# First edge layer of a two-layer graph network: 16-bit keys, and the high part of target blocks compared by a distance from ScalarE

## The chip, the cores and the metric

The kernel runs on one core of a Trainium2 chip. Its engines are TensorE (PE, with its weight loads as PEld), VectorE (DVE), ScalarE (ACT), GpSimd (POOL) and SyncE (SP), and 16 DMA engines move data between the device memory and the on-chip memory. The metric is the time of one execution in microseconds.

## The reference, cut to what matters

There are 50,000 nodes with 256 features and 50,000 edges, each with a source `src`, a target `dst` and one of 8 types. `dst` is sorted when it is drawn.

```python
h = relu(layernorm(x))
xt = einsum('ni,rio->rno', h, weight)             # 8 weights of 256x256
messages = xt[edge_type, dst]                     # row edge_index[1] = dst
x = x + relu(segment_sum(messages, src, 50000) + bias)
h = relu(layernorm(x))
h_neigh = h @ W_neigh                             # keep the 32 largest per row
x = x + h @ W_self + segment_sum(maxk(h_neigh)[src], dst) / max(deg, 1)
```

In the first layer the edge reads the row of `dst` and adds into the row of `src`.

## The kernel before, in words

**Tables.** At the start VectorE makes tables of the edges (lines 783 to 888): for each edge its type, source and target as f32, its code, and the slot that it gets when the edges are ordered by type. There are 400 tiles of 128 slots. `key0` holds for each slot the node to which its message is added (up to 50,000). TensorE turns it, and VectorE copies it from PSUM (line 887) to on-chip memory; SP stores it as `key0_rows` in device memory. `bucket_row` and `high_row` (lines 794 to 796) are `dst >> 7` and `dst >> 9` of every edge in f16, stored as `bucket_rows` and `high_rows`.

**The first edge layer.** It runs in 100 steps of 4 tiles (`NBT`, `B`), two steps per turn of a loop, with buffers for even and odd steps. In the step of batch b:
- SP loads the keys of the batch's 512 slots and the next 128, broadcast to 128 partitions (`load_keys0`, line 530).
- GpSimd gathers the rows of `x` for batch b+3 (`gather0`, line 652) and adds the messages of b into `agg` in device memory (`add0`, line 658), in turns: gather, add, gather, add. An add waits for the add two places before it, and for its message.
- VectorE (`edge0_front`, line 911) compares the row of keys with the column of keys of each tile (`pick`, line 920), makes one-hots for a count of degrees, waits for the gathered rows (line 936), copies the next indices `gidx` (line 937) and computes the statistics of the layer norm. When ScalarE has made `std` (line 1226), it computes the scales; `edge0_cross` (line 942) compares keys with those of the next tile (`cross`, line 947); `edge0_back` makes the scatter's indices.
- ScalarE (`edge0_step`, line 1241), for batch b at step b+2: evicts messages 0, 1 and 2 from PSUM (line 1238) with one turned copy between, then computes `std` and the normalised `h` of batch b+2, then the second turned copy and the last eviction.
- TensorE merges equal keys with `pick`, multiplies by the weight of the tile's type, and adds the part that `cross` carries.

**The counting sort beside it.** The second layer needs the edges in order of `dst`. Its sort is spread over the same steps in phases (`PHASES`, line 471): "hist" 13 steps, "rank" 30 steps with 28 chunks of 14 tiles, "sort" 56 steps and "rest" the last 2. In a rank step SP loads the chunk's rows of `bucket_rows` (f16, 1792 per partition, 128 partitions) and `high_rows` (98 partitions) (`load_rank_rows`, line 535). VectorE's `rank_hots` (line 1008) comes at the end of the step, after front, cross, back and `rank_out`: it compares the high part with the number of the partition (line 1011) for `high_of`, a one-hot over 98 partitions; then 14 comparisons of the bucket row with a column, summed (line 1019). TensorE's `rank_choose` (line 1439) looks up the start of each bucket with `high_of`.

**Order.** The order on each engine is written out by hand: `phased` (line 75) and `pipeline` (line 98) call the parts of a step in order, write out the steps at the edges and put the rest in a loop of two steps. ScalarE's part of the edge layer goes through `pipeline`, the other engines' (but GpSimd's) through `phased`. Semaphores are all counted; `wait_from` skips a wait where there is nothing to wait for yet.

After the edge layer come the node layer (98 steps) and the summing of the second layer, which the change does not touch.

Of the kernel before, what the change touches and what calls it, by code (L numbers as in the profile page):

```python
# [20 lines left out]
F32 = mybir.dt.float32  # L21
F16 = mybir.dt.float16
# [52 lines left out]
def phased(eng, phases, first, last, body):  # L75

    t = 0
    for phase, count, looped in phases:
        lo, hi = max(t + 4, first), min(t + count - 4, last)
        pairs = max(0, (hi - lo) // 2) if looped else 0  # L80
        u = t
        while u < t + count:
            if pairs and u == lo:
                with eng.Fori(0, pairs) as i:
                    body(phase, At(i, lo), At(i, lo - t))
                    body(phase, At(i, lo + 1), At(i, lo + 1 - t))
                u += 2 * pairs
            else:
                body(phase, At(None, u), At(None, u - t))
                u += 1  # L90
        t += count


def inside(b, nb):
    return not isinstance(b, int) or 0 <= b < nb


def pipeline(eng, nb, *parts):

    deepest = max(lag for _, lag in parts)
    first, last = 2 + deepest, nb - 3 + deepest % 2

    def step(i, t):
        for part, lag in parts:
            b = t - lag
            if i is not None:
                part(i * 2 + b, i + b // 2, b % 2)
            elif 0 <= b < nb:  # L110
                part(b, b // 2, b % 2)

    for t in range(first):
        step(None, t)
    with eng.Fori(0, (last + 1 - first) // 2) as i:
        step(i, first)
        step(i, first + 1)
    for t in range(last + 1, nb + deepest):
        step(None, t)


def wait_from(eng, sem, value, batch, first):

    if not isinstance(batch, int) or batch >= first:
        eng.wait_ge(sem, value)
# [18 lines left out]
def graph_layers(nc, x, src, dst, etype, w_rel, bias, w_self, w_neigh, out):  # L144
    agg = nc.dram_tensor("agg", [ROWS, D], F32).ap()
    hs = nc.dram_tensor("hs", [NPAD, D], F32).ap()
    key0_rows = nc.dram_tensor("key0_rows", [(SLOTS + 1) * P], F32).ap()
    bucket_rows = nc.dram_tensor("bucket_rows", [SLOTS * P], F16).ap()
    high_rows = nc.dram_tensor("high_rows", [SLOTS * P], F16).ap()

    ctx = ExitStack()
    with ctx:
        def sb(name, shape, dt=F32):
            return ctx.enter_context(nc.sbuf_tensor(name, shape, dt))

        def sem(name):
            return ctx.enter_context(nc.semaphore(name))
# [51 lines left out]
        rawf = {n: view(zone_b, (3 + k) * COLS, [COLS // P, P]) for k, n in enumerate(NAMES)}  # L209
        tab = {n: sb(f"tab_{n}", [P, COLS]) for n in NAMES}  # L210
        bucket_row = sb("bucket_row", [P, COLS // P, P], F16)
        high_row = sb("high_row", [P, COLS // P, P], F16)
        tmp_i = sb("tmp_i", [P, COLS], I32)
        tmp_f = sb("tmp_f", [P, COLS])
        code16 = sb("code16", [P, COLS], U16)
# [27 lines left out]
        def two(name, shape, dt=F32):  # L243
            return [sb(f"{name}{p}", shape, dt) for p in range(2)]

        def two_views(zone, at, shape, dt=F32):
            words = 1
            for n in shape:
                words *= n
            words = words if dt in (F32, I32) else words // 2  # L250
            return [view(zone, at + p * words, shape, dt) for p in range(2)]
# [4 lines left out]
        msg = two("msg", [P, B * D])  # L256
        pick = [[sb(f"pick{p}{j}", [P, P]) for j in range(B)] for p in range(2)]
        cross = [[sb(f"cross{p}{j}", [P, P]) for j in range(B)] for p in range(2)]
        keyrow = two("keyrow", [P, BE + P])
        gidx = two("gidx", [P, B], I32)  # L260
        sidx = two("sidx", [P, B], I32)
        keycol = two("keycol", [P, B])
# [53 lines left out]
        one_low = two_views(zone_c, DEGREES, [B, P], F16)  # L316
        one_high = two_views(zone_c, DEGREES + B * P, [B, TILES], F16)
        bucket_in = two_views(zone_c, RANK, [RC * P], F16)
        high_in = two_views(zone_c, RANK + RC * P, [RC * P], F16)
        low_pick = two_views(zone_c, RANK + 2 * RC * P, [RC, LO], F16)  # L320
        rank_junk = view(zone_a, 0, [RC, P], F16)
        high_of = two_views(zone_a, RC * P // 2, [RC * P], F16)
# [114 lines left out]
        starts_ready = sem("starts_ready")  # L437
        rank_rows_in = pair("rank_rows_in")
        rank_col = sem("rank_col")
        rank_hot = sem("rank_hot")  # L440
        earlier_done = sem("earlier_done")
        chosenmm = sem("chosenmm")
# [46 lines left out]
        def _(sp):  # L489
# [24 lines left out]
            def store_rows(dram, tile, tiles, done):  # L514
                whole = tiles // P
                v = dram[0:whole * P * P].rearrange("(c r p) -> r c p", r=P, p=P)
                sp.dma_start(v, tile[:, 0:whole, :]).then_inc(done, 16)
                sp.dma_start(dram[whole * P * P:tiles * P].rearrange("(r p) -> r p", p=P),
                             tile[0:tiles - whole * P, whole, :]).then_inc(done, 16)

            sp.wait_ge(rawf_done, 1)
            store_rows(bucket_rows, bucket_row, SLOTS, rank_rows_stored)
            store_rows(high_rows, high_row, SLOTS, rank_rows_stored)
            sp.wait_ge(keyT_done, 1)
            store_rows(key0_rows, rawf["src"], SLOTS + 1, key0_stored)
            sp.wait_ge(key0_stored, 32)
            sp.wait_ge(rank_rows_stored, 64)


            def load_keys0(b, r, p):  # L530
# [3 lines left out]

            def load_rank_rows(c, r, p):
                wait_from(sp, earlier_done, c - 1, c, 2)
                wait_from(sp, rank_hot, c - 1, c, 2)
                at = bass.ds(c * (RC * P), RC * P)
                sp.dma_start(bucket_in[p], bucket_rows[at].unsqueeze(0).to_broadcast([P, RC * P])
                             ).then_inc(rank_rows_in[p], 16)  # L540
                sp.dma_start(high_in[p][0:HI, :], high_rows[at].unsqueeze(0).to_broadcast([HI, RC * P])
                             ).then_inc(rank_rows_in[p], 16)

            def edge0_loads(phase, at, chunk):
# [226 lines left out]
        def _(dve):  # L771
            count = [0]

            def link(ins):

                count[0] += 1
                ins.then_inc(own, 1)
                dve.wait_ge(own, count[0])
# [12 lines left out]
            dve.wait_ge(raw_in, 16 * 9)  # L791
            for n in NAMES:
                link(v.tensor_copy(rawf[n][:, :, :], raw[n][:, :, :]))
            for shift_by, rows16 in ((7, bucket_row), (9, high_row)):
                link(v.tensor_scalar(raw["type"][:, :, :], raw["dst"][:, :, :], shift_by, None, ALU.arith_shift_right))
                link(v.tensor_copy(rows16[:, :, :], raw["type"][:, :, :]))
            v.memset(key0[:, SLOTS:COLS], float(N)).then_inc(rawf_done, 1)
            for k, n in enumerate(NAMES):
                dve.wait_ge(pe_done, k + 1)
# [71 lines left out]
            def decode(coded, to, n):  # L871
# [12 lines left out]
            link(v.tensor_tensor(key0[:, s], key0[:, s], tmp_f[:, s], ALU.add))  # L884
            v.tensor_copy(tmp_f[:, 0:1], key0[:, 0:1]).then_inc(dve_ready, 1)
            dve.wait_ge(pe_done, 5)
            v.tensor_copy(rawf["src"][:, :, :], bank[4][:, :].rearrange("p (c q) -> p c q", q=P)
                          ).then_inc(keyT_done, 1)


# [115 lines left out]
                dve.wait_ge(starts_ready, 1)  # L1006

            def rank_hots(c, rc, p):
                dve.wait_ge(rank_rows_in[p], 32 * (rc + 1))
                wait_from(dve, chosenmm, c - 1, c, 2)  # L1010
                v.tensor_scalar(high_of[p][0:HI, :], high_in[p][0:HI, :], part_f[0:HI, 0:1], None, ALU.is_equal
                                ).then_inc(rank_hot, 1)
                wait_from(dve, rank_own, 4 * (c - 1), c, 2)
                v.tensor_tensor(low_pick[p], iota_h[:, 0:LO].unsqueeze(1).to_broadcast([P, RC, LO]),
                                low16[:, bass.ds(c * RC, RC)].unsqueeze(2).to_broadcast([P, RC, LO]), ALU.is_equal)
                v.tensor_copy(bucket_col[p][:, :], bucket[:, bass.ds(c * RC, RC)]).then_inc(rank_col, 1)
                dve.wait_ge(rank_col, c + 1)
                for j in range(RC):
                    last = v.scalar_tensor_tensor(rank_junk[:, j, :], bucket_in[p][:, j * P:(j + 1) * P],
                                                  bucket_col[p][:, j:j + 1], upto[:, :], ALU.is_equal, ALU.mult,  # L1020
                                                  accum_out=earlier[p][:, j:j + 1])
                last.then_inc(earlier_done, 1)
# [192 lines left out]
        def _(act):  # L1215
# [19 lines left out]
            def edge0_evict(b, p, j):  # L1235
                wait_from(act, added0[j], 16 * (b - 1), b, 2)
                act.wait_ge(msgmm0, b * B + j + 1)
                nc.scalar.copy(msg[p][:, j * D:(j + 1) * D], bank[4 + j % 2][:, j // 2 * D:(j // 2 + 1) * D]  # L1238
                               ).then_inc(msg0, 1)

            def edge0_step(b, r, p):

                turn = not isinstance(b, int) or b + 1 < NBT
                front = not isinstance(b, int) or b + 2 < NBT
                edge0_evict(b, p, 0)
                if turn:
                    edge0_turned(b + 1, 1 - p, 0)
                edge0_evict(b, p, 1)
                edge0_evict(b, p, 2)
                if front:  # L1250
                    edge0_front(b + 2, p)
                if turn:
                    edge0_turned(b + 1, 1 - p, 1)
                edge0_evict(b, p, 3)
# [19 lines left out]
            edge0_turned(0, 0, 0)  # L1274
            edge0_front(1, 1)
            edge0_turned(0, 0, 1)
            pipeline(act, NBT, (edge0_step, 2))


            edge0_over(act)  # L1280
# [315 lines left out]
```

## Time and profile before

| | |
|---|---|
| median of 3 runs | 3609.3 us (3604.76 to 3609.43) |
| the profiled execution | 3607.24 us |
| its span | 3605.5 us |
| busy: DVE, PE, POOL, ACT | 87%, 72%, 68%, 63% |
| mean traffic of the DMA engines | 160 GB/s |
| chain that ended last | DVE 50%, issue 21%, PE 11%, DMA 8% |

The profile is one execution. Busy times are those of each engine over the span, and they overlap. The chain follows, from the last instruction back, what released each piece of work; "issue" is time in which an engine waited for nothing that the profile shows. An idle time before an instruction is put down to what ended it. Times in a timeline are microseconds from the start of the span.

### The profile page before, as it was taken

The numbers are of one execution on the slowest core, as the hardware profiler recorded it, in microseconds if no ns is written. First come the engines' busy times: TensorE is split into PE (matmuls) and PEld (weight loads), VectorE is DVE, ScalarE is ACT, GpSimd is POOL, SyncE is SP. The second block draws the span as 40 slices with busy tenths as digits, with TensorE's granted clock in tenths as the row PEclk, the third lists the DMA queues.
The fourth block names the chain that finished last, engine by engine and source line by source line (L and its number), as shares of the span: only waits on it lengthen the run. The fifth ranks groups of instructions, "written<-read, shape, count | busy, mean of one in ns | idle before, by whom it ended". The sixth has DMA issues, their size and how long they took to land.

```text
span 3605.5 us, 69112 instructions
## 1 busy us (share of the span) xinstructions
PE 2593.9 (72%) x10738; PEld 1677.9 (47%) x10739; DVE 3119.8 (87%) x13785; ACT 2257.1 (63%) x6394; POOL 2450.8 (68%) x1732
## 2 busy tenths in 40 slices
PE   2665666767788888888677777777777765766676
PEld 1224655555566666666333333333333334555454
DVE  8998788888899999999699999999999995666666
ACT  3994233333333333333588888888888867777787
POOL 0003877767787777777688888888888855656665
PEclk9997888888999999999899899998988988889999
DMA  9601466666555555555344444444444437777776
GB/s 368 248 0 48 83 123 144 147 143 149 110 108 104 104 100 103 105 102 100 109 173 164 182 166 171 178 163 177 173 164 182 166 121 244 257 242 258 247 251 218
DMA packets 308041, 576.38 MB, mean 160 GB/s; under 512 B 32095, under 2 KB 188034, under 8 KB 307982
## 3 DMA queue, kind: packets, MB, share of 16 engines
q1 hardware_dynamic: 212366, 419.40, 33.2%
q0 software_dynamic: 95616, 156.31, 22.3%
q8 instruction: 23, 0.38, 0.0%
q14 instruction: 36, 0.29, 0.0%
HBM read 316.70 MB, written 258.88 MB: 160 GB/s over the span
## 4 chain that ended last, share of the span: by engine, by line
DVE 50%; issue 21%; PE 11%; DMA 8%; POOL 4%; DVEq 3%; ACT 2%; POOLq 0%; ACTq 0%; SPq 0%
DVE zone_c L1176 7%; DVE w L1176 7%; DVE best L1169 6%; DVE zone_c L1204 5%; DMA agg<-msg,sidx 5%; PE banks L1569 5%; DMA w<-hs,gidx 3%; PE banks L1469 2%; DVE zone_c L858 2%; DVE zone_c L1049 2%; DVE zone_c L1047 2%; DVE stats L893 2%; DVE zone_c L860 2%; DVE zone_c L1051 2%; POOL rows_in L653 2%
## 5 line engine op out<-in xcount | busy, mean ns | idle before, releaser
L1541 PE MATMUL banks<-w,hT 128*128 128x512 f32 x1568 | 795.4, 666 | 199.8 <-ACT hT L1321 195.1
L665 POOL DMA_INDIRECT agg<-msg,sidx x400 | 665.3, 1663 | 206.4 <-issue 111.9
L653 POOL DMA_INDIRECT rows_in<-in_x,gidx x400 | 421.8, 1054 | 435.7 <-DVE gidx L909 305.3
L1541 PEld LDWEIGHTS banks<-w,hT 128*128 128x128 f32 x1568 | 325.7, 213 | 613.3 <-issue 500.6
L1204 DVE SCALAR_TENSOR_TENSOR zone_c<-banks,rdeg,zone_c 128x256 f32 x784 | 379.4, 484 | 245.8 <-PE banks L1569 201.0
L1569 PE MATMUL banks<-w,zone_c 128*128 x1568 | 428.1, 429 | 208.4 <-DVE zone_c L1204 99.5
L732 POOL DMA_INDIRECT w<-hs,gidx x392 | 371.3, 947 | 230.3 <-DMA w<-hs,gidx 90.6
L1411 PE MATMUL banks<-pick,h 128*128 128x128 f32 x1600 | 287.1, 307 | 311.8 <-ACT h L1220 218.8
L1469 PE MATMUL banks<-w,hT 128*128 x1600 | 481.1, 429 | 18.3 <-issue 17.1
L1238 ACT COPY msg<-banks 128x256 f32<-128x256 f32 x400 | 148.0, 370 | 510.6 <-PE banks L1480 497.3
L1569 PEld LDWEIGHTS banks<-w,zone_c 128*128 128x128 f32 x1568 | 316.1, 212 | 320.6 <-issue 275.2
L1411 PEld LDWEIGHTS banks<-pick,h 128*128 128x128 f32 x1600 | 256.1, 215 | 374.5 <-issue 352.2
L1347 ACT ACTIVATE zone_c<-zone_c,ones 128x128 f32<-128x128 f32 x784 | 305.9, 390 | 134.7 <-PE banks L1569 132.7
L1169 DVE MAX8 best<-zone_c 128x8 f32<-128x256 f32 x980 | 341.9, 411 | 0.0
L1469 PEld LDWEIGHTS banks<-w,hT 128*128 128x128 f32 x1600 | 308.6, 214 | 63.7 <-issue 32.6
L709 POOL TENSOR_TENSOR zone_c<-msg,zone_c 128x1024 f32<-128x1024 f32 x98 | 232.8, 2375 | 149.2 <-ACT zone_c L1309 149.2
L1176 DVE MATCH_REPLACE8 zone_c<-best,zone_c 128x256 f32<-128x256 f32 x784 | 311.9, 409 | 0.0
L1341 ACT ACTIVATE zone_c<-iota_f,minus_key 128x128 f32<-128x128 f32 x784 | 302.6, 386 | 4.7 <-DMA hs<-zone_c 4.6
L698 POOL TENSOR_SCALAR zone_c<-zone_c 128x1024 f32<-128x1024 f32 x98 | 272.0, 2775 | 7.0 <-DMA zone_c<-agg 7.0
L1480 PE MATMUL banks<-msg,cross 128*128 128x256 f32 x798 | 261.4, 412 | 0.0
L1226 ACT ACTIVATE std<-mv,eps 128x4 f32<-128x4 f32 x100 | 29.7, 297 | 345.7 <-DVE mv L897 345.7
L703 POOL TENSOR_TENSOR zone_c<-rows_in,zone_c 128x1024 f32<-128x1024 f32 x98 | 235.6, 2404 | 8.6 <-POOL zone_c L698 0.2
(233 smaller groups left out, 5841.6 us busy)
## 6 DMA issues: line engine op xcount, KB each, us to landing
out_rows<-zone_c SPq DMA_DIRECT2D x196, 512.0 KB, 2.7
agg<-bias SPq DMA_DIRECT2D x2, 25344.0 KB, 97.3
zone_c<-agg SPq DMA_DIRECT2D x98, 512.0 KB, 5.4
hs<-zone_c SPq DMA_DIRECT2D x98, 512.0 KB, 3.6
zone_c<-out_rows SPq DMA_DIRECT2D x98, 512.0 KB, 6.0
rows_in<-in_x SPq DMA_DIRECT2D x97, 512.0 KB, 4.6
keyrow<-key_rows SPq DMA_DIRECT2D x100, 320.0 KB, 4.0
zone_c<-bucket_rows SPq DMA_DIRECT2D x28, 448.0 KB
```

The source lines that it names most:

```text
L653: pool.indirect_dma_start(out=rows_in[p][:, j, :], out_offset=None, in_=x[:, :], in_offset=bass.IndirectOffsetOnAxis(ap=gidx[p][:, j:j + 1 ...
L665: pool.indirect_dma_start(out=agg[:, :], out_offset=bass.IndirectOffsetOnAxis(ap=sidx[p][:, j:j + 1], axis=0), in_=msg[p][:, j * D:(j + 1) ...
L732: pool.indirect_dma_start(out=ring[:, k, :], out_offset=None, in_=hs[:, :], in_offset=bass.IndirectOffsetOnAxis(ap=gidx1[p][:, k:k + 1], a ...
L1169: last = v.max(best[:, j, :], (work if k else neigh)[p][:, j, :])
L1176: last = v.match_replace(work[p][:, j, :], best[:, j, :], (work if k else neigh)[p][:, j, :], NEG)
L1204: ins = v.scalar_tensor_tensor(to, bank[k % 8][:, 0:D], node, to, ALU.mult, ALU.add)
L1341: nc.scalar.activation(near[:, k % 4, :], iota_f[:, 0:P], ACT.Abs, bias=minus_key[:, bass.ds(s, 1)]).then_inc(near1, 1)
L1347: nc.scalar.activation(hot1[:, k % HOTS, :], near[:, k % 4, :], ACT.Relu, bias=ones[:, 0:1], scale=-1.0).then_inc(hot1_done, 1)
L1411: last = mm(bank[j // 2][:, k * P:(k + 1) * P], h[p][:, j, c * P:(c + 1) * P], pick[p][j][:, 0:P], start=True, stop=True)
L1469: last = mm(to, hT[p][:, j // 2, k * P:(k + 1) * P], w0[:, bass.ds(rel, 1), c, :].rearrange("k r d -> k (r d)"), start=(c == 0), stop=alon ...
L1541: last = mm(bank[4 + j][:, :], hT[p][:, c, j * P:(j + 1) * P], w1[:, c, :], start=(c == 0), stop=(c == KC - 1))
L1569: mm(bank[k % 8][:, 0:D], hot1[:, k % HOTS, :], ring_cols[:, bass.ds(words[k], D)], start=True, stop=True).then_inc(steps1, 1)
```

## The change

- `key0_rows` and both `keyrow` buffers hold unsigned 16-bit integers. The copy from PSUM writes a new tile `key16`. The load per step is half as many bytes; the comparisons at lines 920 and 947 read 16-bit input, and their outputs stay f32.
- `high_row`, `high_rows` and the load of it are gone. In its place ScalarE computes |bucket - (4 p + 1.5)| from the bucket row on 98 partitions (`rank_distance`), with a per-partition bias `high_mid`, and VectorE compares it with 2: a bucket belongs to the high part p when it is 4p, ..., 4p+3.
- `rank_distance` stands in ScalarE's step between the third eviction and `edge0_front`. VectorE waits for it in `rank_hots`. SP waits for it (`rank_near`), in place of VectorE's comparison, before it loads over a bucket row. ScalarE waits for the bucket row and for the comparison two chunks back.
- ScalarE's edge layer goes through `phased`, so that it knows the chunk; its last step is written behind it.

```diff
-    key0_rows = nc.dram_tensor("key0_rows", [(SLOTS + 1) * P], F32).ap()
+    key0_rows = nc.dram_tensor("key0_rows", [(SLOTS + 1) * P], U16).ap()
-    high_rows = nc.dram_tensor("high_rows", [SLOTS * P], F16).ap()
-        high_row = sb("high_row", [P, COLS // P, P], F16)
+        high_mid = sb("high_mid", [P, 1])
+        key16 = sb("key16", [P, COLS // P, P], U16)
-        keyrow = two("keyrow", [P, BE + P])
+        keyrow = two("keyrow", [P, BE + P], U16)
-        high_in = two_views(zone_c, RANK + RC * P, [RC * P], F16)
+        high_near = two_views(zone_c, RANK + RC * P, [RC * P], F16)
...
-            store_rows(high_rows, high_row, SLOTS, rank_rows_stored)
             sp.wait_ge(keyT_done, 1)
-            store_rows(key0_rows, rawf["src"], SLOTS + 1, key0_stored)
+            store_rows(key0_rows, key16, SLOTS + 1, key0_stored)
...
             def load_rank_rows(c, r, p):
                 wait_from(sp, earlier_done, c - 1, c, 2)
-                wait_from(sp, rank_hot, c - 1, c, 2)
+                wait_from(sp, rank_near, c - 1, c, 2)
                 at = bass.ds(c * (RC * P), RC * P)
                 sp.dma_start(bucket_in[p], bucket_rows[at].unsqueeze(0).to_broadcast([P, RC * P])
-                             ).then_inc(rank_rows_in[p], 16)
-                sp.dma_start(high_in[p][0:HI, :], high_rows[at].unsqueeze(0).to_broadcast([HI, RC * P])
                              ).then_inc(rank_rows_in[p], 16)
...
-            for shift_by, rows16 in ((7, bucket_row), (9, high_row)):
-                link(v.tensor_scalar(raw["type"][:, :, :], raw["dst"][:, :, :], shift_by, None, ALU.arith_shift_right))
-                link(v.tensor_copy(rows16[:, :, :], raw["type"][:, :, :]))
+            link(v.tensor_scalar(raw["type"][:, :, :], raw["dst"][:, :, :], 7, None, ALU.arith_shift_right))
+            link(v.tensor_copy(bucket_row[:, :, :], raw["type"][:, :, :]))
+            v.tensor_scalar(high_mid[:, :], part_f[:, :], -float(LO), -(LO - 1) / 2, ALU.mult, ALU.add)
...
-            v.tensor_copy(rawf["src"][:, :, :], bank[4][:, :].rearrange("p (c q) -> p c q", q=P)
+            v.tensor_copy(key16[:, :, :], bank[4][:, :].rearrange("p (c q) -> p c q", q=P)
...
             def rank_hots(c, rc, p):
-                dve.wait_ge(rank_rows_in[p], 32 * (rc + 1))
+                dve.wait_ge(rank_rows_in[p], 16 * (rc + 1))
                 wait_from(dve, chosenmm, c - 1, c, 2)
-                v.tensor_scalar(high_of[p][0:HI, :], high_in[p][0:HI, :], part_f[0:HI, 0:1], None, ALU.is_equal
-                                ).then_inc(rank_hot, 1)
+                dve.wait_ge(rank_near, c + 1)
+                v.tensor_scalar(high_of[p][0:HI, :], high_near[p][0:HI, :], LO / 2, None, ALU.is_lt).then_inc(rank_hot, 1)
...
+            def rank_distance(c, rc, p):
+                act.wait_ge(rank_rows_in[p], 16 * (rc + 1))
+                wait_from(act, rank_hot, c - 1, c, 2)
+                nc.scalar.activation(high_near[p][0:HI, :], bucket_in[p][0:HI, :], ACT.Abs, bias=high_mid[0:HI, 0:1]
+                                     ).then_inc(rank_near, 1)
+
-            def edge0_step(b, r, p):
+            def edge0_step(b, p, chunk):
...
                 edge0_evict(b, p, 2)
+                if chunk is not None:
+                    rank_distance(*chunk)
                 if front:
                     edge0_front(b + 2, p)
...
-            pipeline(act, NBT, (edge0_step, 2))
+
+            def edge0_body(phase, at, chunk):
+                b, _, p = at.back(2)
+                c, rc, pc = chunk.back(0)
+                if inside(b, NBT):
+                    edge0_step(b, p, (c, rc, pc) if phase == "rank" and inside(c, RCHUNKS) else None)
+
+            phased(act, PHASES, 2, NBT, edge0_body)
+            edge0_step(NBT - 1, 1, None)
```

## Rows read from the trace of the kernel before

**Rows 1.** Busy us by stretch (start:end, length), engines; then PEclk, DMA share, GB/s.
```profile
520.00:930.00 410.00, 286.14 (x1589) 236.42 (x1590) 349.19 (x2146) 132.78 (x305) 290.64 (x219) 0.84 0.68 146
930.00:1640.00 710.00, 586.19 (x3048) 450.50 (x3047) 645.63 (x3421) 254.81 (x584) 557.45 (x428) 0.94 0.57 104
```

**Rows 2.** Timeline of DVE, line 937, rank: start, us, instruction, [idle before <-what ended it].
```profile
528.94 0.16 DVE L937 COPY gidx<-from 128x4 int32<-128x4 int32 x1
...
756.97 0.17 DVE L937 COPY gidx<-from 128x4 int32 x1 [4.07 <-DMA rows_in<-in_x,gidx]
...
918.87 0.17 DVE L937 COPY gidx<-from 128x4 int32<-128x4 int32 x1 [1.40 <-DMA rows_in<-in_x,gidx]
```

**Rows 3.** Waits in rank (first), then hist: total us, times, longest.
```profile
DVE gidx L937 <- DMA rows_in<-in_x,gidx: 27.9, 24, 4.1
...
DVE pick L920 <- DMA keyrow<-key_rows: 15.3, 4, 5.8
```

**Rows 4.** Timeline of one rank step, picked from SP, POOL, DVE and ACT.
```profile
698.31 0.33 SPq L532 DMA_DIRECT2D keyrow<-key_rows  x1
699.00 0.33 SPq L539 DMA_DIRECT2D zone_c<-bucket_rows  x1
699.13 1.66 POOL L665 DMA_INDIRECT agg<-msg,sidx  x1 [0.30 <-issue]
...
704.43 1.02 POOL L653 DMA_INDIRECT rows_in<-in_x,gidx  x1 [0.30 <-issue]
708.79 1.58 POOL L665 DMA_INDIRECT agg<-msg,sidx  x1 [3.33 <-DMA agg<-msg,sidx]
709.31 0.17 DVE L937 COPY gidx<-from 128x4 int32 x1 [1.15 <-DMA rows_in<-in_x,gidx]
...
711.35 0.30 ACT L1226 ACTIVATE std<-mv,eps 128x4 f32<-128x4 f32 x1 [4.02 <-DVE mv L897]
```

**Rows 5.** Chain of waits over 520 to 940: shares by line; one piece (start, us).
```profile
by line: DMA agg<-msg,sidx 35.8%; issue 25.9%; POOL rows_in L653 10.6%; PE banks L1469 7.1%; POOL agg L665 6.5%; PE banks L1411 4.1%; PE banks L1480 3.1%; DMA rows_in<-in_x,gidx 1.5%; ACT h L1220 1.3%; PE banks L1419 1.0%; DVE stats L893 0.
...
699.13 8.74 DMA agg<-msg,sidx
```

**Rows 6.** Timeline of POOL in sort, two adds two places apart.
```profile
1203.10 1.58 POOL L665 DMA_INDIRECT agg<-msg,sidx  x1 [0.30 <-issue]
...
1210.05 1.64 POOL L665 DMA_INDIRECT agg<-msg,sidx  x1 [0.30 <-issue]
```

**Rows 7.** Busy time of a short stretch in rank, columns as in rows 1.
```profile
700.00:707.00 7.00, 7.00 (x34) 5.54 (x34) 6.91 (x47) 1.37 (x4) 4.54 (x4) 0.79 0.99 234
```

**Rows 8.** DMA in rank: SP's queue (packets, MB, share); the key load's us to landing.
```profile
q1 hardware_dynamic: 10944, 31.05, 27.7%
...
keyrow<-key_rows SPq DMA_DIRECT2D x28, 320.0 KB, 4.5
```

**Rows 9.** Groups of DVE's instructions in rank: busy us, mean ns of one.
```profile
L1019 DVE SCALAR_TENSOR_TENSOR zone_a<-zone_c,bucket_col,upto 128x128 f16<-128x128 f16 x392 | 109.2, 347 | 1.0
...
L920 DVE SCALAR_TENSOR_TENSOR pick<-keyrow,keycol,upto 128x128 f32<-128x128 f32 x110 | 32.2, 348 | 1.9 <-DVE keycol L915 0.5
...
L947 DVE TENSOR_SCALAR_CACHE_REDUCE cross<-keyrow,livekey 128x128 f32<-128x128 f32 x110 | 31.6, 343 | 1.3
L927 DVE TENSOR_SCALAR zone_c<-iota_h,lowcol 128x128 f16<-128x128 f16 x108 | 27.7, 256 | 0.0
```

**Rows 10.** Groups of ACT's instructions over the span: busy us, mean ns of one.
```profile
L1341 ACT ACTIVATE zone_c<-iota_f,minus_key 128x128 f32<-128x128 f32 x784 | 302.6, 386 | 4.7 <-DMA hs<-zone_c 4.6
...
L1329 ACT ACTIVATE w<-w,minus_one 128x512 f32<-128x512 f32 x98 | 70.8, 722 | 50.2 <-DVE w L1176 47.0
```

**Rows 11.** ACT in rank: its wait before `std` in total, and the shortest in the timeline.
```profile
ACT std L1226 <- DVE mv L897: 94.4, 27, 7.3
...
530.97 0.30 ACT L1226 ACTIVATE std<-mv,eps 128x4 f32<-128x4 f32 x1 [1.29 <-DVE mv L897]
```

**Rows 12.** Timeline of DVE near the start.
```profile
10.87 0.43 DVE L796 CAST high_row<-zone_b 128x512 f16<-128x512 int32 x1
```

More of the change, by code:

```diff
@@ L439, in graph_layers @@
         rank_col = sem("rank_col")
+        rank_near = sem("rank_near")
         rank_hot = sem("rank_hot")
@@ L522, in _ @@
             store_rows(bucket_rows, bucket_row, SLOTS, rank_rows_stored)
-            store_rows(high_rows, high_row, SLOTS, rank_rows_stored)
             sp.wait_ge(keyT_done, 1)
-            store_rows(key0_rows, rawf["src"], SLOTS + 1, key0_stored)
+            store_rows(key0_rows, key16, SLOTS + 1, key0_stored)
             sp.wait_ge(key0_stored, 32)
-            sp.wait_ge(rank_rows_stored, 64)
+            sp.wait_ge(rank_rows_stored, 32)
             def load_keys0(b, r, p):
```

## Prediction

> **What bounds the kernel now.** I read the page first, then the busy time by stretch, with the first edge layer cut at its phases. Tables are built until 313 us; then come "hist" (to about 520), "rank" (to about 930), "sort" (to about 1640) and a short rest. Rank and sort are what the reader should compare [rows 1]. Each of rank's 28 chunks loads two kinds of bucket rows, which sort doesn't. Vector and GpSimd are both close to their limit there, so the question is which wait ends last.
>
> The distance between the copies of `gidx` gives one step: in rank, from 528.94 to 918.87 in 26 steps, 15.0 us each [rows 2]. Vector waits 27.9 us in 24 places for gathered rows of `x` [rows 3]. GpSimd issues four gathers and four scatter-adds per step. In the step shown [rows 4] an add starts at 699.13, the one two places on at 708.79, after an idle time of 3.33 us that a scatter ended: an add waits for the one two places back. The gather at 704.43 lands late behind the same traffic, and Vector waits for it until 709.31. The chain of waits agrees: the largest entry of the rank stretch is scatters under way, 35.8%, and the piece in that step runs 8.74 us from start to landing [rows 5]. In sort, two adds that are two places apart start 6.95 us apart, and no scatter ends the idle time before the later one [rows 6]. So rank is bound by scatters that land late, with Vector near behind; sort is bound by Vector, which is busy for 645.6 of 710 us [rows 1].
>
> Why late? SP issues the key load at 698.31, the buckets at 699.00 and then the high parts [rows 4], just ahead of the slow scatter. From 700 to 707 the DMA engines are 99% busy at 234 GB/s [rows 7], against 68% over the stretch [rows 1]. Burst and scatter share the engines.
>
> **The high rows go, and the keys halve.** In rank SP's queue moved 31.05 MB in 27.7% of 410 us [rows 8]: 113.6 us of all engines, 3.66 us per MB. The high load is 98 rows of 3584 bytes, 0.351 MB: 1.28 us. Half of the keys' 320 KB is 0.164 MB: 0.60 us. Together 1.88 us leave each burst, of the 4.2 us that its three loads (1.14 MB) cost. The scatter of 8.74 us would land after 6.9 if it moves by the whole of that. GpSimd itself needs an add, a gather and two issue gaps, twice, between two such adds: 2 x (1.58+0.30+1.00+0.30) = 6.4 us [rows 4, 6]. So most of a stall of 2 to 3 us goes, about 1.9 us in a period of 15.0. Next late is Vector: its step without the gather wait is 15.0 - 27.9/26 = 13.9 us, and there the gain stops. Bounds: 27.9 us, and nothing, if the scatter is late for another reason. I take 24 us, since the longest wait, 4.07 us [rows 2], exceeds what 1.9 us take off, and a few like it leave some 4 us.
>
> In hist Vector waits 15.3 us in four places for keys [rows 3]. That is latency more than volume: keys land after 4.5 us in rank [rows 8], of which the halved bytes are 0.60. Four times 0.6 is 2.4; I take 2, bounds 0 and 15.3. In sort I take 0: its steps are bound by Vector's own work.
>
> **Compares on 16-bit keys.** `pick` (L920) takes 348 ns with f32 input; the same instruction at L1019 with 16-bit input and output takes 347 [rows 9]. So 0. For `cross` (L947, 343 ns) no row shows a 16-bit form. The nearest single-input compare with 16-bit on both sides is L927, 256 ns, without a sum. Bounds: 0, and 400 x 0.087 = 35 us less. I take 0, since the output and the sum stay f32 and L1019 gains nothing even with both sides at 16-bit.
>
> **The distance on ScalarE.** ACT takes 386 ns for 128 elements and 722 for 512 [rows 10]: 0.875 ns each, so 1792 elements take 722 + 1280 x 0.875 = 1842 ns. It stands after the third eviction and ahead of `std`, for which Vector waits; the normalising of `h`, a turned copy and the fourth eviction are queued behind it, and PE and GpSimd's fourth add wait for those. ACT sits idle just there: 94.4 us in rank's 27 steps, 3.5 in the mean, 1.29 in the shortest [rows 11], the only one of them under 1.84. That costs 0.55 us once; I take 1 for all, since steps that were held up by gathers lose some cover. The distance needs its bucket row, issued at 699.00, for the idle time that begins at 711.35 - 4.02 = 707.33 [rows 4], 8.3 us later; keys land in 4.5 [rows 8]. Vector's new wait for the distance comes after its wait for `std`, which follows the distance on ACT: no stall. SP's wait for the distance two chunks back ends before the wait beside it (`earlier_done`), so its queue, keys included, isn't delayed; it issues one DMA less. If the cover is gone, each step costs up to 1.84 us.
>
> The Trainium skill ("ScalarE: Activation LUTs", Rules for kernel authors) advises keeping simple arithmetic off ScalarE, which it puts at up to three times slower per element. The formula in its section What ACT_TABLE_LOAD costs gives an estimate of 1.77 us for this instruction, near the 1.84 from the rows. By the rule the edit is a loss, at most the rival of the late `std` below; the trace speaks against it here, since the idle time hides the length.
>
> **Rank's compare.** L1011 keeps shape and types, with a number in place of a [98,1] operand, and one wait instruction more. I take 0; as bounds, an estimate of the 87 ns between L947 and L927 for either way, 28 x 0.087 = 2.4 us less or more.
>
> **The start.** A shift and a cast of 128x512 go, 0.43 us each [rows 12], and a [128,1] operation comes, well under half of one. Vector works alone for most of the time up to 313 us: -0.8 us, bounds -0.9 and -0.5. The key store, in half the bytes but in runs of 256 bytes instead of 512, stands before the first key load: 0, bounds -1 and +1. ScalarE's loop is written out per phase as the other engines' are; ACT is busy 132.8 of 410 us [rows 1], which hides it: 0, at worst +3 at the edges of phases.
>
> **Sum.** -24 - 2 - 0.8 + 1 = -26 us. The profiled execution took 3607.24 us, span 3605.5, and would take 3581. The median of the runs shown, 3609.3, lies 2 us above it, so I forecast 3583 us.
>
> **Rivals.**
> - *The volume was not the cause.* The scatter stands behind the bucket load, which stays, or GpSimd's own order keeps it late. For it: the larger of the row loads keeps its place. Against: the burst loses 45% of its bytes. Kept are the start and some of the rest, 1 to 7 us: 3605. Chance 0.15.
> - *The distance delays `std`* (the slower side). A bucket row that lands late puts the distance in front of `std`. It decides at 711.35 - 1.84 = 709.5, 10.5 us after the issue: every microsecond beyond costs one per step. Full price 28 x 1.84 = 52 us, less the 26 gained: 3635; it is slower than before once over half of each distance is exposed. For it: the burst still fills the engines to 707. Against: 3.5 us of mean idle time, and fewer bytes ahead. Chance 0.07.
> - *`cross` gets faster.* Up to 35 us on Vector; GpSimd's period of 4 x 3.18 = 12.7 us lies under Vector's by enough to let most of it through. Some 30 more: 3553. For it: a compare at 256 ns exists. Against: L1019. Chance 0.08.
> - *The forecast*, with its own range of 3574 to 3595. Chance 0.70.
>
> Less than about 0.2%, 7.2 us, can't be told from no change. Faster by more: 0.70 + 0.08 + 0.02 of the first rival = 0.80. Same: 0.12 of the first rival. Slower: 0.07 + 0.01 = 0.08. The range takes in the first rival up to 3604 and reaches toward the third: 3565 to 3604.
>
> **What would show it.** Right: hardly any idle time of GpSimd in rank that a scatter ends; Vector's gather wait there below 6 us; steps of 13.9 to 14.1 us with the chain through Vector; a distance of 1.8 us inside ACT's idle time; L920 and L947 unchanged; sort as long as before. Wrong: scatters still over 7 us from start to landing; Vector waiting longer for `std`; L947 under 300 ns. The forecast fails above all if the scatters' landing doesn't move.

## The result and the profile after

| | before | after |
|---|---|---|
| median | 3608.2 us (3604.8 to 3609.4, 4 runs) | 3575.1 us (3574.6 to 3576.8, 4 runs) |
| ratio, 95% interval | | 0.9911 [0.9893, 0.9928] |
| span of the profiled execution | 3605.5 us | 3573.5 us |
| mean granted clock of TensorE | 0.904 | 0.906 |

The change makes the kernel faster, by 0.9%. 3583 us was forecast, 8 us above the result, which lies in the range. The page of after has the same engines at the top. In the chain that ended last the DMA engines have 3% and Vector 57% (8% and 50% before), and the key load is half as large.

```profile
DVE 57%; issue 20%; PE 11%; DVEq 4%; DMA 3%; POOL 2%; ACT 2%; POOLq 0%; ACTq 0%; SPq 0%
...
keyrow<-key_rows SPq DMA_DIRECT2D x100, 160.0 KB, 3.6
zone_c<-bucket_rows SPq DMA_DIRECT2D x28, 448.0 KB, 5.3
```

Busy time of after in rank and in sort, columns as in [rows 1]. The stretch taken for rank is 27 us shorter, its ends rounded to fit each trace; Vector does the same work in it (347 us) and is now busy for 91% of it, against 85%. The DMA share falls from 0.68 to 0.61.

```profile
520.00:903.00 383.00, 279.10 (x1582) 231.45 (x1583) 346.87 (x2128) 176.41 (x328) 290.42 (x222) 0.86 0.61 120
903.00:1612.00 709.00, 592.45 (x3090) 455.10 (x3089) 647.14 (x3451) 256.54 (x587) 561.90 (x428) 0.94 0.54 92
```

Waits of after in rank (total us, times, longest). The wait for gathered rows, 27.9 us in [rows 3], is 0.5. GpSimd waited 32.3 us in 13 places for scatters before; now 2.0 in two. What holds an add back now is its message from ScalarE (28.4 us; 22.9 before).

```profile
DVE gidx L935 <- DMA rows_in<-in_x,gidx: 0.5, 1, 0.5
...
POOL agg L663 <- DMA agg<-msg,sidx: 2.0, 2, 1.1
...
POOL agg L663 <- ACT msg L1236: 28.4, 30, 1.7
...
ACT std L1224 <- DVE mv L895: 28.3, 21, 2.7
...
DVE rstd L900 <- ACT std L1224: 10.2, 27, 0.7
```

The chain through rank, by line. In [rows 5] scatters under way were its largest entry, 35.8%; they aren't among the entries that the line shows any more, and Vector's lines lead.

```profile
by line: DVE zone_a L1017 18.2%; issue 14.5%; DVE stats L891 7.2%; PE banks L1483 6.8%; DVE pick L918 6.5%; DVE cross L945 6.4%; DVE zone_c L926 5.4%; PE banks L1425 4.4%; DVE zone_c L925 3.5%; PE banks L1494 3.2%; DVE mv L895 2.1%; ACT std
```

A rank step of after, picked from four engines; compare [rows 4]. The distance (L1242) ends at 796.42, 0.81 us before `std` begins, so it lies in idle time. The add at 801.62 waits for its message, not for a scatter.

```profile
794.63 1.79 ACT L1242 ACTIVATE zone_c<-zone_c,high_mid 98x1792 f16<-98x1792 f16 x1
...
795.18 0.17 DVE L935 COPY gidx<-from 128x4 int32 x1
...
797.23 0.30 ACT L1224 ACTIVATE std<-mv,eps 128x4 f32<-128x4 f32 x1 [0.81 <-DVE mv L895]
...
799.32 0.33 SPq L532 DMA_DIRECT2D keyrow<-key_rows  x1
...
801.62 1.73 POOL L663 DMA_INDIRECT agg<-msg,sidx  x1 [1.37 <-ACT msg L1236]
```

Vector's instructions in rank that read the keys, and the compare of the distance (busy us, mean ns). They answer to [rows 9]: 349 for 348 ns, and 343 for 343. L1010, with a number in place of a [98,1] operand, took 694 ns before.

```profile
L918 DVE SCALAR_TENSOR_TENSOR pick<-keyrow,keycol,upto 128x128 f32<-128x128 uint16 x108 | 31.7, 349 | 1.4
L945 DVE TENSOR_SCALAR_CACHE_REDUCE cross<-keyrow,livekey 128x128 f32<-128x128 uint16 x108 | 31.0, 343 | 1.2
L1010 DVE TENSOR_SCALAR zone_a<-zone_c 98x1792 f16<-98x1792 f16 x28 | 17.8, 635 | 2.8 <-issue 0.4
```

**Where 32 us of span went.** The copies of `gidx`, one per step and numbered here from 0, are landmarks in both traces. After leads by 1.3 us at the first, by 1.2 at number 13 (the first step of rank), by 25.6 at number 41 (behind rank's last chunk), by 29.9 at 43 (the first step of sort) and by 32.7 at the last. So hist gave nothing, rank's chunks 24.4 us, the two steps from 41 to 43, with neither a chunk of rank nor one of sort, 4.2, the rest of the edge layer some 3, and what follows it nothing (the lead is 32.0 at the end). The stretches called sort in [rows 1] and above begin ahead of these two.

### The profile page after: what moved, and what is told of

Its sections match the earlier page's. It is cut to its first block, busy times and chain, and to the rows that moved or that the text cites. A ratio compares the mean times of both kernels' runs of the same rounds, so it can differ in the third digit from the quotient of the medians.

```text
span 3573.5 us, 69007 instructions
## 1 busy us (share of the span) xinstructions
PE 2582.5 (72%) x10738; PEld 1668.3 (47%) x10739; DVE 3115.5 (87%) x13784; ACT 2306.0 (65%) x6422; POOL 2444.8 (68%) x1732
## 3 DMA queue, kind: packets, MB, share of 16 engines
q0 software_dynamic: 95616, 156.31, 22.9%
## 4 chain that ended last, share of the span: by engine, by line
DVE 57%; issue 20%; PE 11%; DVEq 4%; DMA 3%; POOL 2%; ACT 2%; POOLq 0%; ACTq 0%; SPq 0%
DVE zone_c L1174 7%; DVE w L1174 7%; DVE best L1167 6%; DVE zone_c L1202 5%; PE banks L1583 4%; DVE stats L891 3%; PE banks L1483 3%; DMA w<-hs,gidx 3%; DVE pick L918 3%; DVE cross L945 2%; DVE zone_c L1045 2%; DVE zone_c L926 2%; DVE zone_c L856 2%; DVE zone_c L1047 2%; DVE zone_c L1049 2%
## 5 line engine op out<-in xcount | busy, mean ns | idle before, releaser
L1218 ACT ACTIVATE h<-rows_in,shift,rstd 128x256 f32<-128x256 f32 x400 | 207.3, 588 | 44.2 <-DVE shift L902 44.2
```

## The experiments

Each run is compared with the kernel before on the same chip. From the last copy of `gidx` to the end, which no edit touches, the traces take 1890 to 1980 us, so only ratios and stretches are compared across chips. "Rank" is the mean of 22 steps between copies of `gidx` (numbers 17 to 39); "turn" is the next six steps, from rank's last two chunks into sort; "sort" is the mean of 50 steps (46 to 96). Each is read from one trace; the two of the changed kernel differ by 0.03 us a step in rank, 0.5 in the turn and 0.02 in sort.

| run | ratio to before | rank, us a step | turn, us | sort, us a step |
|---|---|---|---|---|
| before | | 14.94 | 83.3 | 13.36 |
| after | 0.9911 [0.9893, 0.9928] | 14.14 | 77.9 | 13.30 |
| a0_after | 0.9916 [0.9898, 0.9934] | 14.11 | 77.4 | 13.28 |
| k1_keys_only | 0.9988 [0.9979, 0.9997] | 14.89 | 82.3 | 13.32 |
| k2_distance_only | 0.9917 [0.9903, 0.9930] | 14.19 | 77.8 | 13.18 |
| k9_full_traffic | 0.9991 [0.9977, 1.0005] | 15.04 | 82.8 | 13.30 |
| k8_own_rows | 0.9982 [0.9970, 0.9994] | 14.86 | 83.3 | 13.32 |
| k3_load_put_back | 0.9935 [0.9922, 0.9949] | 14.48 | 81.0 | 13.16 |
| k11_half_load | 0.9951 [0.9934, 0.9968] | 14.55 | 83.1 | 13.24 |
| k10_rows_later | 0.9920 [0.9898, 0.9942] | 14.18 | 78.1 | 13.34 |
| k12_rows_later_keys16 | 0.9931 [0.9915, 0.9948] | 14.18 | 77.6 | 13.33 |
| k5_distance_twice | 0.9965 [0.9951, 0.9978] | 14.75 | 80.2 | 13.20 |
| k6_distance_last | 1.0053 [1.0035, 1.0071] | 15.82 | 82.6 | 13.22 |
| k7_bucket_col_on_act | 0.9925 [0.9907, 0.9942] | 13.94 | 77.2 | 13.47 |

**Which part: the keys alone.** The kernel before with 16-bit keys and nothing else.

```diff
-    key0_rows = nc.dram_tensor("key0_rows", [(SLOTS + 1) * P], F32)
+    key0_rows = nc.dram_tensor("key0_rows", [(SLOTS + 1) * P], U16)
...
-        keyrow = two("keyrow", [P, BE + P])
+        keyrow = two("keyrow", [P, BE + P], U16)
...
```

> The kernel before with 16-bit keys alone: the load of the high rows and its comparison on VectorE stay. Theory A (the bytes of the burst of loads delay one scatter-add per rank step): 0.60 of the 1.88 us of DMA time per burst goes, so GpSimd's idle time on scatters in rank falls by about a third from 55 us (scatter and message together), Vector's wait for gathered rows from 27.9 to about 17 us, and the whole kernel is 8 to 14 us faster, 3 of it at the start of the sort phase. Rival B (only the third load, behind the buckets, is what the scatter stands behind): rank keeps its 15.0 us steps, and no more than 4 us are gained. Rival C (16-bit input speeds the comparison of the sort phase): the sort phase is over 10 us shorter and L947 is under 330 ns.

Some 4 us of 3660, and rank's steps hardly move. Its waits in 310 us of rank (560 to 870) show the stall still there. The first fence is of this run, the second of before in the same stretch.

```profile
POOL agg L666 <- DMA agg<-msg,sidx: 20.1, 9, 3.5
...
DVE gidx L938 <- DMA rows_in<-in_x,gidx: 17.7, 17, 3.4
```

```profile
POOL agg L665 <- DMA agg<-msg,sidx: 26.5, 11, 3.3
...
DVE gidx L937 <- DMA rows_in<-in_x,gidx: 19.9, 18, 4.1
```

**Which part: the distance alone.** After, with keys as f32 again (the diff above the other way round).

> The changed kernel with f32 keys again: the high rows are not loaded, ScalarE makes the distance. Theory A: 1.28 of 1.88 us of DMA time per burst goes, enough to take the scatter's landing under the 6.4 us that GpSimd needs anyway in most steps: rank steps of 14.0 to 14.3 us, Vector's gather wait under 8 us, 20 to 28 us faster than before. Rival B (the third load is all): the same rank stretch as in the changed kernel, 24 us less than before, and the keys' part is only in the start of sort. Rival D (gains need both parts, since the wait vanishes only under a threshold): under 12 us faster.

It gives as much as the whole change, and the same two waits are all but gone:

```profile
DVE gidx L934 <- DMA rows_in<-in_x,gidx: 0.7, 1, 0.7
...
POOL agg L662 <- DMA agg<-msg,sidx: 3.5, 3, 1.2
```

**After again**, on the chip of k8_own_rows, k9_full_traffic and k7_bucket_col_on_act.

> The changed kernel again, beside the runs with parts of it, so that ratios and stretches stand on one chip. Every theory: 0.989 to 0.993 of the time before, rank steps (17 to 39) of 14.1 to 14.2 us, as in the two profiles compared so far.

0.9916 on another chip, with rank at 14.11: the result holds.

**The load put back, without its use.** After, and SP loads 98 x 1792 numbers into a tile that nobody reads, from `bucket_rows`; Vector waits for them.

```diff
+                sp.dma_start(unread[p][0:HI, :], bucket_rows[at].unsqueeze(0).to_broadcast([HI, RC * P])
+                             ).then_inc(unread_in[p], 16)
...
+                dve.wait_ge(unread_in[p], 16 * (rc + 1))
```

> The changed kernel with one more load per rank chunk, 98 rows of 3584 bytes as the high rows were, right behind the bucket load, into a tile that nothing reads; VectorE waits for its landing where it waits for the bucket row. Theory A (bytes in the burst): GpSimd's idle time on scatters comes back, rank steps rise from 14.0 to 14.5 or more, and the kernel is 12 to 22 us slower than the changed one, so 11 to 21 us faster than the one before. Rival E (what helped was not the load but the shorter comparison with a number, 59 ns, or ScalarE's new loop): within 3 us of the changed kernel.

Rank 14.48: under half of the 0.75 us that k1_keys_only has over after. Either ScalarE's part has a worth of its own, or this load isn't the old one. It reads the rows that the load just ahead of it reads.

**The same load from rows of its own.** As the last, with a second copy of the bucket rows stored at the start.

```diff
-                sp.dma_start(unread[p][0:HI, :], bucket_rows[at].unsqueeze(0).to_broadcast([HI, RC * P])
+                sp.dma_start(unread[p][0:HI, :], high_rows[at].unsqueeze(0).to_broadcast([HI, RC * P])
...
```

> As the one with a load put back, but the load that nothing reads comes from rows of its own in device memory, as the high rows did, so its three loads move the same bytes between the same places as those of the kernel with 16-bit keys alone, whose rank steps took 14.89 us; with the load from the bucket rows they took 14.48. Theory G (where the bytes come from matters: a second read of the same rows is cheaper): 14.8 to 14.9 us a step, 8 to 10 us slower than the load from the bucket rows. Theory H (it doesn't; what separates 14.48 from 14.89 is who compares, and when VectorE and ScalarE run): 14.4 to 14.6 us again.

14.86, as in k1_keys_only with the same traffic and no distance. SP's queue (packets, MB, share of 16 engines over 310 us of rank), k3_load_put_back first and then this run:

```profile
q1 hardware_dynamic: 8719, 21.19, 23.0%
```

```profile
q1 hardware_dynamic: 8400, 20.45, 26.3%
```

That is 0.230 x 310 / 21.19 = 3.36 us of all engines per MB, against 3.99, for the whole of SP's queue. The two runs differ only in the rows that the third load reads and in the store of them at the start, so reading the same rows again was the cheaper load, 14.48 against 14.86 us a step. How it is cheaper is not shown: the time per MB is not the load's own price, for k10_rows_later below, whose loads all read rows of their own, has 0.268 x 310 / 24.76 = 3.36 as well.

**The whole traffic of before, with the distance.** As the last, with f32 keys.

> The changed kernel with f32 keys and the load that nothing reads from rows of its own: the loads of the kernel before, byte for byte, with the distance on ScalarE. Theory A in its strict form (the bytes of the burst alone set rank's steps): 14.9 to 15.1 us a step, within 4 us of the kernel before. Theory H (a part of the gain is not bytes): 14.6 to 14.7 us a step, 6 us or more faster than before.

Ratio 0.9991, and its interval holds 1; rank 15.04. With the bytes back the gain is gone, so it came from the load that left, and the distance costs or gives less than this can tell. Halving the keys beside the full load is worth 15.04 - 14.86 = 0.18 us a step with the distance and 14.94 - 14.89 = 0.05 without it; once the load is out, 14.19 - 14.11 = 0.08.

**Half of the load.** k8_own_rows with 49 partitions in place of 98.

> The changed kernel with the load that nothing reads from rows of its own, on 49 partitions instead of 98: half the dose of the kernel that had 14.86 us a rank step, against 14.13 with none. Linear in bytes: 14.5 us. Threshold (a landing that stays under the 6.4 us which GpSimd needs anyway costs nothing): 14.1 to 14.25 us, and idle time of GpSimd on scatters under 5 us between 560 and 870, against 23.1 with the full load.

14.11 with none, 14.55 with half, 14.86 with all: each half costs, the first 0.44 us and the second 0.31. Half of the load is not under a size that would be free; smaller loads were not tried.

**All the bytes, later in the step.** The kernel before with one edit: SP waits until Vector has ended the comparisons of the chunk before, not those of two chunks back, so the row loads go out some 7 us after the keys and not 0.7.

```diff
-                wait_from(sp, earlier_done, c - 1, c, 2)
-                wait_from(sp, rank_hot, c - 1, c, 2)
+                wait_from(sp, earlier_done, c, c, 1)
```

> The kernel before, all its loads kept, but SP issues the two loads of a rank chunk only when VectorE has ended the comparisons of the chunk before (earlier_done at c in place of c - 1): at 704.8 instead of 699.0 in the step shown, so after the scatter of 699.13 instead of ahead of it. They would land 7.6 us later at 712.4, before their use at 714.9. Theory A (any burst of these bytes makes some scatter of the step late, and every scatter has the same 6.4 us): the stall moves to another add, steps of 14.8 to 15.1 us, within 6 us of before. Theory I (it is the place of the burst against this one scatter): steps of 14.1 to 14.4 us, 16 to 24 us faster, with no byte less. Over 15.2 us would say that VectorE now waits for the rows.

Not a byte is saved, and rank takes 14.18 us a step; the ratio is 0.9920, beside 0.9911 and 0.9916 for the change. The timeline shows the new place, with two adds already under way:

```profile
690.03 0.33 SPq L532 DMA_DIRECT2D keyrow<-key_rows  x1
...
693.03 1.58 POOL L664 DMA_INDIRECT agg<-msg,sidx  x1 [0.30 <-issue]
...
696.94 0.33 SPq L538 DMA_DIRECT2D zone_c<-bucket_rows  x1
697.37 0.37 SPq L540 DMA_DIRECT2D zone_c<-high_rows  x1
...
703.72 1.58 POOL L664 DMA_INDIRECT agg<-msg,sidx  x1 [1.26 <-DMA agg<-msg,sidx]
```

GpSimd still waits for scatters in 310 us of rank, 14.4 us for 26.5 before, but never for more than 1.8 us, and Vector has no wait for gathered rows in this stretch at all. SP's queue moves as many bytes as before:

```profile
POOL agg L664 <- DMA agg<-msg,sidx: 14.4, 12, 1.8
```

```profile
q1 hardware_dynamic: 8703, 24.76, 26.8%
```

**Both remedies.** k10_rows_later with 16-bit keys; ScalarE makes no distance.

> The kernel before with two edits: the wait ahead of the two loads of rank rows is the later one of k10_rows_later, and the keys are 16-bit numbers as in k1_keys_only. All three loads stay, and ScalarE makes no distance. Theory I (what counts is where the burst stands against the scatter-add): rank steps of 14.1 to 14.2 us, as k10_rows_later had (14.18); the keys, which stay in their early place with half the bytes, take another 0 to 0.1 us a step off and some 1 to 4 us at the start of sort, as in k1_keys_only: ratio to before 0.989 to 0.992. It beats the changed kernel (0.9911 and 0.9916 in its two comparisons) only if it comes to 0.990 or less; I expect no difference that can be told. Theory B (the bytes taken out are what counts, and k10_rows_later gained by something else): 14.14 or less in rank from the keys' bytes alone, 13.95 at best, since Vector's own step is near; ratio 0.988.

Rank 14.18 again and 0.9931: no gain on the change or on k10_rows_later, whose intervals overlap with this one. In 310 us of rank Vector has no wait for gathered rows in any of the three, and at most 8.0 us for `std`: rank goes at about Vector's own pace.

**The distance twice.** After, with the activation once more into a tile that nobody reads, just ahead.

```diff
+                nc.scalar.activation(near_junk[0:HI, :], bucket_in[p][0:HI, :], ACT.Abs, bias=high_mid[0:HI, 0:1])
                 nc.scalar.activation(high_near[p][0:HI, :], bucket_in[p][0:HI, :], ACT.Abs, bias=high_mid[0:HI, 0:1]
```

> The changed kernel with the distance made twice, the first into a tile that nothing reads. It tests the cover on ScalarE ahead of std: after the change 28.3 us of idle time are left there in 21 of rank's 27 steps, 1.3 us each. Theory A (the cover is idle time ahead of std, and what goes beyond it is paid in full): the second distance, 1.79 us, is exposed for about 0.5 us in the steps with cover and more in the others, so 12 to 30 us slower than the changed kernel, and Vector's wait for std grows from 10.2 us by that. Rival F (Vector has other slack, a late std is made up for by a wait that ends anyway): under 5 us slower.

Of the second 1.79 us, 14.75 - 14.11 = 0.64 a step shows: a third. Vector's wait for `std` in 310 us of rank is 8.0 us in after; here it is 20.0, some 0.6 us a step more, which is what the step has lost. GpSimd waits a little longer for messages (25.9 us in after):

```profile
DVE rstd L901 <- ACT std L1225: 20.0, 20, 1.9
...
POOL agg L664 <- ACT msg L1237: 30.8, 22, 2.3
```

**The distance last in ScalarE's step**, behind the fourth eviction.

```diff
                 edge0_evict(b, p, 2)
-                if chunk is not None:
-                    rank_distance(*chunk)
...
                 edge0_evict(b, p, 3)
+                if chunk is not None:
+                    rank_distance(*chunk)
```

> The changed kernel with the distance after the fourth eviction instead of ahead of std. In a step of the changed kernel that eviction ends at 800.77 and VectorE reaches its comparison at 801.13, so it would wait for a distance that ends at 802.6: 1.5 us a step, rank steps of 15.3 to 15.8 us, 35 to 45 us slower than the changed kernel and slower than before. If instead std had been held up by the distance where it stands now, the earlier std would give some of that back and the steps stay under 15.0 us.

The same 1.79 us, moved, cost 15.82 - 14.14 = 1.7 us a step, and the kernel is slower than before. In 310 us of rank, some 20 steps, Vector waits 1.5 us a step for the distance (30.8 / 20), and GpSimd waits for messages:

```profile
DVE zone_a L1010 <- ACT zone_c L1242: 30.8, 20, 2.1
...
POOL agg L663 <- ACT msg L1236: 62.3, 33, 2.9
```

**Vector lighter by 0.17 us.** After, with the copy of `bucket_col` on ScalarE.

```diff
-                v.tensor_copy(bucket_col[p][:, :], bucket[:, bass.ds(c * RC, RC)]).then_inc(rank_col, 1)
...
+                wait_from(act, earlier_done, c - 1, c, 2)
+                nc.scalar.copy(bucket_col[p][:, :], bucket[:, bass.ds(c * RC, RC)]).then_inc(rank_col, 1)
```

> The changed kernel with the copy of 14 columns (bucket_col, 0.17 to 0.3 us on VectorE per rank step) made by ScalarE, ahead of the distance, in the idle time that is left there. If VectorE now bounds rank, its steps lose 0.1 to 0.25 us, 3 to 7 us in all, as long as ScalarE's idle time ahead of std (1.3 us a step) covers 0.25 us more. If a wait on another engine bounds rank: no change within 2 us.

Rank falls by that 0.17, to 13.94, as it would where Vector sets the step. The 5 us of 28 steps don't show in the time (0.9925 beside 0.9916, within the intervals); in its trace the sort steps took 13.47 us, which no edit explains.

## Why the prediction was right, and where it wasn't

- **The stall and its cause: right.** Rank was held by scatters that land behind SP's burst. Forecast were 24 us for rank, measured 24.4 with steps of 14.1; both waits went, and the chain turned to Vector. k2_distance_only and k9_full_traffic show that the load's removal does it.
- **The 24 us: right in size, in part by luck.** The prediction left some 4 us of the gather wait standing; 0.5 are left. Yet Vector's idle time in rank fell only from 410 - 349.2 = 60.8 us to 383 - 346.9 = 36.1, by 24.7. The two errors nearly offset each other, and where the missing 2.7 us of idle time stand is open.
- **How far the scatter's landing moves: mis-sized.** Forecast were 8.74 - 1.88 = 6.9 us. By the landing events of the traces (560 to 870 us), the add that stood right behind the burst, one of the four in a step, takes 7.5 us from start to landing in the mean before and 3.9 after; the slowest of the four then takes 4.9, and none over 6.3. With the keys alone it is 7.4, with half of the load 6.9, and with the later rows the slowest add takes 5.8. So the landing moved by 3.6 us and not by the 1.88 us of engine time that left. In after the add next to the burst also starts later behind the bucket load, 1.73 us in the step shown and not 0.13, so part of this is the place and not the volume.
- **The share by bytes: mis-sized.** The prediction took 1.88 us from each burst, of which the keys had 0.60, a third. On the chip the keys are worth 0.05 to 0.18 us of the 0.8 a step. The keys go out first and the rows stand next to the slow scatter; that this is the reason was not tested. The division did not enter the total, since the high rows alone bring rank down to about Vector's own step, where the prediction had the gain stop.
- **The step from "the burst fills the engines" to "fewer bytes": not the only way.** k10_rows_later kept every byte and had nearly all of the gain. The rival that the volume isn't the cause had 0.15 and was priced with no gain in rank. It was half true: the place matters too. But the load's removal had the gain all the same.
- **Keys in hist: wrong.** 2 us forecast, none came: the key waits fell from 15.3 to 13.5 us, and the gather waits in the same steps rose from 21.6 to 23.0. The next wait stood right behind: 1.8 us less in the one, 1.4 more in the other.
- **Between rank's last chunk and sort's first: missed.** Nothing was forecast for the two steps there, 4.2 us came. Before, Vector still waited 1.46 us for gathered rows in each, and after in neither; the waits for keys fell from 3.53 and 1.59 us to 2.23 and 1.83. Together that is 2.9 + 1.1 = 4.0. The turn is 82.3 us with the keys alone and 77.8 with the distance alone, so most of it comes from the rows' load, though neither step loads rows. GpSimd fits this: before, it has no pause over 0.31 us between its DMAs from 918.45, where it had last waited for a scatter, to 959, so it is still catching up. The first fence is of before, the second of after.

```profile
941.98 0.35 DVE L920 SCALAR_TENSOR_TENSOR pick<-keyrow,keycol,upto 128x128 f32<-128x128 f32 x1 [3.53 <-DMA keyrow<-key_rows]
...
946.53 0.17 DVE L937 COPY gidx<-from 128x4 int32<-128x4 int32 x1 [1.46 <-DMA rows_in<-in_x,gidx]
...
958.55 0.17 DVE L937 COPY gidx<-from 128x4 int32<-128x4 int32 x1 [1.46 <-DMA rows_in<-in_x,gidx]
```

```profile
915.01 0.35 DVE L918 SCALAR_TENSOR_TENSOR pick<-keyrow,keycol,upto 128x128 f32<-128x128 uint16 x1 [2.23 <-DMA keyrow<-key_rows]
```

- **The distance: right.** 1.79 us measured for 1.84 forecast, hidden ahead of `std`: Vector waits 10.2 us there in rank, 9.8 before. k6_distance_last shows that the same instruction at another place is a loss. The Trainium skill ("ScalarE: Activation LUTs", Rules for kernel authors) says to use VectorE and not ScalarE for simple arithmetic such as `add` or `max`. Taken as a rule for the time, it is not borne out at the first place, where rank's steps fell, and is at the second. The estimate of 1.77 us from the formula in that page's section What ACT_TABLE_LOAD costs was slightly closer than the 1.84 from the rows.
- **Compares on 16-bit keys: right at nothing.** 349 and 343 ns.
- **Rank's compare: small gain missed.** 694 - 635 = 59 ns times 28, 1.7 us, within the bounds given.
- **The start: 1.3 us for 0.8.** 0.85 us is the shift and the cast, less the small new operation; Vector's wait for the first keys is 5.4 us and not 5.8.
- **The rest of sort:** about 3 us that were not forecast. Steps of sort vary from 13.16 (k3_load_put_back) to 13.47 us (k7_bucket_col_on_act) with the same code, so these 3 us can't be put down to the change. What they come from stays open.

## What to carry to other kernels

When an indirect scatter lands late, look at what was issued just ahead of it. Here, moving the burst by 6 us within the step gave what taking a load out gave, at the price of one changed wait. Price a load by where it stands, not by its share of the bytes, and stop counting where the next engine's own step begins. Work moved to another engine is covered where that engine waits for its next input anyway and the result is wanted later: the same 1.8 us showed no cost in one place and cost 1.7 in another.

## What the runs showed of the hardware

- A scatter-add started within about a microsecond behind a burst of 1.14 MB landed after 7.5 us in the mean, other adds of the same steps after 3.8 to 5.1; with 45% of the burst left out no add took over 6.3 (before, after).
- An unread load that reads the same rows again right after a first load cost the step less than one from rows of its own, 14.48 against 14.86 us (k3_load_put_back, k8_own_rows). SP's queue took 3.36 us of all engines per MB against 3.99, but also 3.36 with rows of their own in another place of the step (k10_rows_later).
- Compares with a sum (128x128) took the same time from unsigned 16-bit as from f32 input: 349 and 343 ns, for 348 and 343 (after, before).
- A plain compare of 98x1792 in 16 bits took 635 ns with a number and 694 with a per-partition operand (after, before), though the comparison itself differs too (less-than for equal).
